# A top-k attention stage: loads split, masked probabilities as a difference of two exponentials, scores in two pairs, weights one turn later

## The reference, cut to what matters

```python
K_TOP = 32                                   # H = 4 heads of DH = 32
Q = (x_text @ Wq).reshape(Bb, Tt, H, DH)     # Tt = 112
K = (x_vision @ Wk).reshape(Bb, Gg, H, DH)   # Gg = 375
scores = jnp.einsum('bthd,bghd->bhtg', Q, K) / np.sqrt(DH).astype(np.float32)
scores = jnp.where(vision_mask[:, None, None, :], scores, -jnp.inf)
topv, topi = jax.lax.top_k(scores, K_TOP)
probs = jax.nn.softmax(topv, axis=-1)
attn = jnp.zeros_like(scores).at[bi, hi, ti, topi].set(probs)
attn_mean = attn.mean(axis=1)
V = x_vision @ Wv
c_t = jnp.einsum('btg,bgd->btd', attn_mean, V)
c_t = c_t * text_mask[..., None]
```

## Time and profile before

| | us |
|---|---|
| median of three runs | 2866.13 |
| the runs | 2863.48 to 2870.03 |
| the profiled execution | 2862.95 |
| its span, first to last instruction | 2861.2 |
| busy in the span: TensorE, Vector engine, ScalarE, GpSimd | 2240.2, 1638.0, 690.7, 736.3 |
| mean granted clock of TensorE | 0.849 of full speed |

### The profile page before, as it was taken

How to read it: one execution, slowest core, us unless ns; L and a number is a source line. 1 busy time by engine, 2 the same in 40 slices (tenths; PEclk the granted TensorE clock), 3 DMA queues, 4 the chain that set the end, 5 groups by cost and what they waited for, 6 DMA issues and landing times.

```text
span 2861.2 us, 36958 instructions
## 1 busy us (share of the span) xinstructions
PE 2240.2 (78%) x14996; PEld 1512.3 (53%) x14996; DVE 1638.0 (57%) x3176; ACT 690.7 (24%) x1321; POOL 736.3 (26%) x667
## 2 busy tenths in 40 slices
PE   4444589899987999699999999988656765775776
PEld 1111245555555666578888888777444543343432
DVE  5888844444443333355555555566298896645335
ACT  4222123223221121122222222222122221211122
POOL 1222269524130000334343434332200001101000
PEclk8666689788887899899999999999756576887888
DMA  2000010000001000100000100100140011300000
GB/s 84 0 0 0 17 66 14 9 9 9 9 13 45 0 1 1 70 1 1 37 22 1 58 1 1 43 1 1 51 93 28 25 33 31 72 19 0 0 0 26
DMA packets 49704, 64.14 MB, mean 22 GB/s; under 512 B 30856, under 2 KB 46976, under 8 KB 48384
## 3 DMA queue, kind: packets, MB, share of 16 engines
q1 hardware_dynamic: 49536, 61.78, 7.4%
HBM read 59.71 MB, written 2.06 MB: 22 GB/s over the span
## 4 chain that ended last, share of the span: by engine, by line
PE 67%; DVE 20%; DMA 4%; POOL 3%; ACT 3%; issue 2%; SPq 1%; POOLq 0%; DVEq 0%; ACTq 0%
PE PS L1200 7%; PE PS L1216 7%; PE PS L617 4%; DVE st_h L478 4%; PE PS L957 4%; PE PS L936 3%; PE PS L1117 3%; DMA ctx_k<-in_ctx 3%; PE PS L1722 3%; DVE st_h L487 2%; PE PS L643 2%; PE PS L1837 2%; PE PS L628 2%; PE PS L656 2%; DVE ln_st L260 2%
## 5 line engine op out<-in xcount | busy, mean ns | idle before, releaser
L279 POOL TENSOR_SCALAR ln_ve<-ln_mv 128x2 f32<-128x2 f32 (+1 forms) x95 | 21.1, 222 | 1631.0 <-DVE ln_mv L263 1630.9
L1392 DVE TENSOR_TENSOR p_x<-PS,cols 128x1024 f32<-128x1024 f32 x112 | 129.3, 1217 | 147.8 <-PE PS L1162 147.8
L333 PE MATMUL PS<-bc_parts,ident 96*128 96x448 bf16 x256 | 88.2, 438 | 159.7 <-DVE st_h L487 149.7
L1454 POOL TENSOR_TENSOR q_x<-q_f,cols 128x2048 f32<-128x2048 f32 x56 | 208.5, 3743 | 9.9 <-ACT q_f L1312 9.9
L800 DVE TENSOR_REDUCE XD<-PS 112x2 f32<-112x750 f32 x128 | 120.3, 940 | 130.8 <-PE PS L643 130.7
L643 PE MATMUL PS<-k_s,q_s 32*112 32x375 f32 x512 | 130.6, 565 | 42.0 <-DVE XD L800 41.2
L769 ACT ACTIVATE e_t<-PS 125x672 f32<-125x672 f32 x128 | 93.6, 731 | 256.3 <-PE PS L656 256.2
L333 PEld LDWEIGHTS PS<-bc_parts,ident 96*128 96x128 bf16 x256 | 22.1, 107 | 235.3 <-DVE st_h L487 192.7
L1021 DVE SCALAR_TENSOR_TENSOR XA<-PS,gate_w,XA 112x256 f32<-112x256 f32 x128 | 61.9, 484 | 135.4 <-PE PS L957 135.4
L530 POOL TENSOR_TENSOR st_h<-st_h 128x448 f32<-128x448 f32 x64 | 71.9, 1135 | 248.8 <-DVE st_h L487 248.4
L656 PE MATMUL PS<-q_s,k_s 32*125 32x112 f32 x1536 | 128.7, 301 | 1.1 <-ACT e_t L769 1.1
(11 more groups left out here) (337 smaller groups left out, 5006.0 us busy)
## 6 DMA issues: line engine op xcount, KB each, us to landing
t_ring<-k_scratch SPq DMA_DIRECT2D x8, 784.0 KB, 12.5
enc_w<-in_enc_w SPq DMA_DIRECT2D x2, 3072.0 KB, 10.0
wc<-in_enc_w SPq DMA_DIRECT2D x2, 3072.0 KB, 11.9
ctx_k<-in_ctx SPq DMA_DIRECT2D x16, 281.2 KB
wc<-in_wc SPq DMA_DIRECT2D x1, 4096.0 KB, 14.6
enc_rows<-in_enc_rows SPq DMA_DIRECT2D x4, 896.0 KB, 12.3
XD<-k_scratch SPq DMA_DIRECT2D x4, 784.0 KB, 9.1
ctx_t<-in_ctxT SPq DMA_DIRECT2D x16, 187.5 KB, 2.4
```

The source lines that it names most:

```text
L333: last = pe.matmul(ps[2 * (j % 2) + m][:, 0:QT], ident16[0:96, s:s + 1].to_broadcast([96, P]), bc_parts[0:96, q * QT:(q + 1) * QT], start= ...
L1392: last = dve.tensor_tensor(p_x[:, m, :, :, :], ps[1][:, m * P:(m + 1) * P].rearrange("p (h i) -> p h i", i=16).unsqueeze(2) .to_broadcast( ...
L1454: last = pool.tensor_tensor(q_x[:, c, :, :].rearrange("p t (h i) -> p t h i", i=16), q_f[:, k % 2, c, :].rearrange("p (t i) -> p t i", i=1 ...
```

## The change

It does the following.

- **Loads.** `features(b)` issues the two `ctx_f` loads on semaphores of their own. They wait for the keys of b - 2, and stand one batch ahead of `ctx_k` in the queue. `keys` waits for `ctx_f` alone, and the second product for `ctx_k`. Five tap tables are loaded in the stage and eleven after it, with the slots in another order.
- **Probabilities.** The Vector engine no longer multiplies. ScalarE computes `e_r`, the exponentials of what turn 3 left in `w_s` (where the 32 marked ones come out as zero), and the exponentials of the 32 found values in `top8`, with their sum in `e_sum`. GpSimd subtracts `e_r` from `e_p`, which leaves the 32 probabilities. `w_s` and `top8` have a place for each head.
- **Weights.** The reciprocal and the scaling of batch b - 1 (`weights`) stand in turn 1 of batch b's first pair, and the diagonals (`spread`) behind the first two exponentials of b.
- **Order on TensorE.** scores(b+1) for heads 0 and 1, context(b-1), scores(b+1) for heads 2 and 3, keys(b+2), then values.

The diff, with most of the unchanged lines left out:

```diff
@@ -145,9 +145,9 @@
         k_e = sb("k_e", [P, 2, S2], pool=s4a)
-        w_s = sb("w_s", [T, 2, S2], pool=s4a)
         e_p = sb("e_p", [T, 2 * XH, S2], pool=s4a)
-        top8 = sb("top8", [T, 2, 4, 8], pool=s4a)
+        top8 = sb("top8", [T, XH, 4, 8], pool=s4a)
+        e_top = sb("e_top", [T, 2, 32], pool=s4a)
         neg_m = sb("neg_m", [T, 4], pool=s4a)
...
@@ -166,6 +166,9 @@
         s4x.close()
+        flat_b = wb[:, :, :].rearrange("p k d -> p (k d)")
+        w_s = flat_b[0:T, 0:XH * S2].rearrange("t (h s) -> t h s", h=XH)
+        e_r = wc[0:T, 5250 + T:5250 + T + 2 * S2].rearrange("t (z s) -> t z s", z=2)
         m1 = XD
...
@@ -181,8 +184,8 @@
             a[0:T, 0:TD * T].rearrange("p (i t) -> p i t", t=T)
-            for a in (wb[:, :, :].rearrange("p k d -> p (k d)"), wc[:, 6144:8192], flat_d[:, 0:TD * T],
-                      flat_d[:, TD * T:2 * TD * T])]
+            for a in (wc[:, 6144:8192], flat_d[:, 0:TD * T], flat_d[:, TD * T:2 * TD * T],
+                      wb[:, :, :].rearrange("p k d -> p (k d)"))]
         SLOTS_T = len(t_slots)
...
@@ -1599,13 +1602,16 @@
         t_loaded = [(sem(f"t_loaded{i}"), 0) for i in range(4)] + [
-            (enc_loaded[0], 64), (enc_loaded[1], 64), (ctx_loaded[0], 16 * B), (ctx_loaded[1], 16 * B)]
+            (enc_loaded[0], 64), (enc_loaded[1], 64), (ctx_loaded[0], 32 * B), (ctx_loaded[1], 32 * B)]
         (m_ready, m_used, x_s_ready, x_first, x_exp, x_rs, x_dg, fi_ready, fi_used, x2_normed, x2_affine,
...
             "g_done f2x_ready f2x_added").split())
+        x_cut, CUT_0 = max_done, PAIRS
+        x_total, SUM_0 = exp_done, PAIRS
+        x_masked, MASKED_0 = pair_added, 8 * len(UNITS)
         S4_ROWS = ("g_in", "b_in", "bf_in", "bf_out", "g_ffn", "b_ffn", "b2", "g_out", "b_out")
...
@@ -1635,34 +1641,43 @@
                 .then_inc(em_loaded, 16)
+
+            def features(b):
+                if b >= 2:
+                    sp.wait_ge(m_ready, m_count("k", b - 2) + 1)
+                for i in range(2):
+                    sp.dma_start(ctx_f[0:CR[i], b % 2, i, :], dr["ctxT"][b, i * P:i * P + CR[i], :])\
+                        .then_inc(ctx_loaded[b % 2], 16)
+
+            features(0)
             for b in range(B):
+                if b + 1 < B:
+                    features(b + 1)
                 if b >= 2:
                     sp.wait_ge(m_ready, m_count("m1", b - 2) + 1)
-                for i in range(2):
-                    sp.dma_start(ctx_f[0:CR[i], b % 2, i, :], dr["ctxT"][b, i * P:i * P + CR[i], :])\
-                        .then_inc(ectx_loaded[b % 2], 16)
                 sp.dma_start(ctx_k[:, b % 2, :, :], dr["ctx"][b].rearrange("(j p) f -> p j f", p=JR))\
...
                     sp.wait_ge(k_stored, 16)
-                    for j in range(6):
+                    for j in range(5):
                         sp.dma_start(t_slots[j], toeplitz(j)).then_inc(t_loaded[j][0], 16)
             sp.wait_ge(m_ready, len(M_AT))
-            for j in range(6, TAPS):
+            for j in range(5, TAPS):
                 if j >= SLOTS_T:
...
         def m_uses():
-            uses = [("q", q) for q in range(NQ)] + [("k", 0)]
-            for b in range(B):
-                if b + 1 < B:
-                    uses.append(("k", b + 1))
-                uses += [("at", b), ("m1", b)]
-                if b % QB == QB - 1:
-                    uses += [("ct", 2 * (b // QB)), ("ct", 2 * (b // QB) + 1)]
+            uses = [("q", q) for q in range(NQ)] + [("k", 0), ("k", 1)]
+            for b in range(B + 1):
+                if b >= 1:
+                    uses += [("at", b - 1), ("m1", b - 1)]
+                if b + 2 < B:
+                    uses.append(("k", b + 2))
+                if b % QB == 0 and b >= 1:
+                    uses += [("ct", 2 * (b // QB) - 2), ("ct", 2 * (b // QB) - 1)]
             return {u: n for n, u in enumerate(uses)}
...
@@ -1695,15 +1710,15 @@
                 bank = m_claim(pe, "k", b)
-                pe.wait_ge(ectx_loaded[b % 2], 48 * (b // 2 + 1))
+                pe.wait_ge(ctx_loaded[b % 2], 32 * (B // 2 + b // 2 + 1))
                 for i in range(2):
...
-            def scores(b):
+            def scores(b, h0):
                 pe.wait_ge(m_used, m_count("k", b) + 1)
-                for h in range(XH):
+                for h in (h0, h0 + 1):
                     n = XH * b + h
...
@@ -1717,6 +1732,7 @@
                 pe.wait_ge(x_dg, b + 1)
+                pe.wait_ge(x_masked, MASKED_0 + XH * (b + 1))
                 for j in range(JC):
...
@@ -1725,6 +1741,7 @@
                 pe.wait_ge(m_used, m_count("at", b) + 1)
+                pe.wait_ge(ectx_loaded[b % 2], 16 * (b // 2 + 1))
                 for i in range(2):
...
@@ -1742,14 +1759,20 @@
             keys(0)
-            scores(0)
-            for b in range(B):
+            keys(1)
+            scores(0, 0)
+            scores(0, 2)
+            for b in range(B + 1):
                 if b + 1 < B:
-                    keys(b + 1)
-                    scores(b + 1)
-                context(b)
-                if b % QB == QB - 1:
-                    values(b // QB)
+                    scores(b + 1, 0)
+                if b >= 1:
+                    context(b - 1)
+                if b + 1 < B:
+                    scores(b + 1, 2)
+                if b + 2 < B:
+                    keys(b + 2)
+                if b % QB == 0 and b >= 1:
+                    values(b // QB - 1)
...
@@ -1885,26 +1908,50 @@
-            copy_keys(0)
-            copy_keys(1)
-            for b in range(B):
-                for h in range(XH):
-                    n = XH * b + h
-                    act.wait_ge(x_first, n + 1)
-                    if b >= 2 and h == 0:
-                        act.wait_ge(m_ready, m_count("at", b - 2) + 1)
-                    act.activation(e_p[:, XH * (b % 2) + h, :], ps[h][0:T, 0:S2], ACT.Exp,
-                                   bias=neg_m[:, h:h + 1]).then_inc(x_exp, 1)
-                    if b >= 1 and h == 1:
-                        copy_attention(b - 1)
-                        copy_context(b - 1)
-                        if b + 1 < B:
-                            copy_keys(b + 1)
+            def exp_all(b, h):
+                n = XH * b + h
+                act.wait_ge(x_first, n + 1)
+                if b >= 2 and h == 0:
+                    act.wait_ge(m_ready, m_count("at", b - 2) + 1)
+                act.activation(e_p[:, XH * (b % 2) + h, :], ps[h][0:T, 0:S2], ACT.Exp,
+                               bias=neg_m[:, h:h + 1]).then_inc(x_exp, 1)
+
+            def exp_rest(b, h):
+                n = XH * b + h
+                act.wait_ge(x_cut, CUT_0 + n + 1)
+                if n >= 2:
+                    act.wait_ge(x_masked, MASKED_0 + n - 1)
+                    act.wait_ge(x_total, SUM_0 + 2 * (n - 1))
+                act.activation(e_r[:, n % 2, :], w_s[:, h, :], ACT.Exp, bias=neg_m[:, h:h + 1]).then_inc(x_total, 1)
+                act.activation(e_top[:, n % 2, :], top8[:, h, :, :].rearrange("t k j -> t (k j)"), ACT.Exp,
+                               bias=neg_m[:, h:h + 1], accum_out=e_sum[:, b % 2, h:h + 1]).then_inc(x_total, 1)
+
+            def spread(b):
                 act.wait_ge(x_rs, b + 1)
...
                 last.then_inc(x_dg, 1)
+
+            copy_keys(0)
+            copy_keys(1)
+            for b in range(B):
+                exp_all(b, 0)
+                exp_all(b, 1)
+                if b >= 1:
+                    spread(b - 1)
+                exp_rest(b, 0)
+                exp_rest(b, 1)
+                exp_all(b, 2)
+                exp_all(b, 3)
+                if b >= 1:
+                    copy_attention(b - 1)
+                    copy_context(b - 1)
+                if b + 2 < B:
+                    copy_keys(b + 2)
+                exp_rest(b, 2)
+                exp_rest(b, 3)
+            spread(B - 1)
             copy_attention(B - 1)
...
@@ -1933,8 +1980,14 @@
             dve.wait_ge(xa_copied, B // 2)
+
+            def weights(b):
+                dve.wait_ge(x_total, SUM_0 + 2 * XH * (b + 1))
+                link(dve.reciprocal(e_rs[:, b % 2, :], e_sum[:, b % 2, :]))
+                dve.tensor_scalar(e_rs[:, b % 2, :], e_rs[:, b % 2, :], tmk[:, b:b + 1], 1.0 / XH,
+                                  ALU.mult, ALU.mult).then_inc(x_rs, 1)
+
             for b in range(B):
-
                 for h0 in range(0, XH, 2):
...
@@ -1947,32 +2000,29 @@
                                 link.after(cut[a])
-                            s = ps[h][0:T, 0:S2] if turn == 0 else w_s[:, a, :]
-                            found[a] = link.mark(dve.max(top8[:, a, turn, :], s))
+                            s = ps[h][0:T, 0:S2] if turn == 0 else w_s[:, h, :]
+                            if turn == 0 and b >= 1:
+                                dve.wait_ge(x_total, SUM_0 + 2 * (n - 3))
```

(28 more changed lines are left out.)

## The result

| | before | after |
|---|---|---|
| median of four runs, us | 2866.88 | 2844.64 |
| the runs, us | 2863.48 to 2870.03 | 2841.04 to 2847.66 |
| ratio to before (95% interval) | | 0.9922 (0.9904 to 0.9941) |
| the profiled execution, us | 2862.95 | 2847.12 |

What follows compares the result with a forecast made beforehand. A DMA chained to TensorE's whole batch work bounded the kernel at 20.9 us a step. Fifteen steps of 18.3, 16.6 for the last batch and 13.2 for values gave 304.3 against 330.1, net -24.2: 2842 us, range 2812 to 2866.

Steps and rivals of the forecast that it cites:

- The load left the chain: Scoring stage: with loads split, the DMA and its issues leave the chain of waits, 6.2 us of a step.
- The masks left the Vector engine: Vector engine, each pair of heads: the mask-and-sum of 1.05 us is removed, with its wait for ScalarE.
- its floor of 16.4 us a batch: Vector engine's own work per batch if nothing else waits: two pairs at 7.99 us plus 0.42 for reciprocal and scaling.
- the price of two heads' scores: TensorE, a pair of heads' scores in the loop: 1.45 us at the full clock, 1.9 at the low one.
- the ring: Loop from `weights` to the next through Vector engine, ScalarE and TensorE: 15.8 us at 2.4 GHz, 19.0 at 1.2 GHz.
- The weighted sum on the chain in most steps: Scoring stage, a sign that the forecast is wrong: most steps wait for the weighted sum, behind `x_masked`.
- 0 to 3 us of waiting a step: Vector engine, a sign that the forecast is right: its waits, all at `weights`, for ScalarE.
- Values: Batches 4, 8 and 12: values' matmuls 3.83 us and last copy 0.53 on the loop, 4.4 each, 13.2 us in all.
- The last batch: End of the scoring stage: 16.6 us, plus 1.1 for the weighted sum beginning later after the last replacement.
- Half the steps at each clock: Scoring steps: half at 16.4 us (full clock), half at 19.0 (low), each plus 0.6; 18.3 us on average.
- The hold: GpSimd's subtraction delaying `neg_m` and `weights`: 0 to 1.3 us a step, 0.6 taken; rival with larger holds, chance 0.10.
- the earlier start: Start of the scoring stage: forecast +0.5 us, waiting for two key products instead of one but for a shorter load.

Runs made afterwards that it cites:

- the last kernel: Changed kernel with four heads' scores between weighted sum and second product, keys' and values' copies late, and values spread over two batches: 2792.78 us, ratio 0.9728.
- The four-head kernel: Changed kernel with the scores of all four heads in one piece behind context(b-1), instead of two pairs: 2825.16 us, ratio 0.9856.
- all of it: Changed kernel with four heads' scores in one piece and the copies of keys and values behind exp_rest: 2808.96 us, ratio 0.9806.

## Why the prediction was right, and where it was wrong

**Right.** The load left the chain: none of the DMAs is waited for, and `features(3)` was issued at 2092.6 us (forecast near 2096). The masks left the Vector engine, and its floor of 16.4 us a batch stands, as the last kernel shows. MAX8 and the replacements keep their 0.53 to 0.54 us beside GpSimd. A pair of `exp_rest` takes 1.7 us (forecast 1.75, with the sum's read at 0.19 us where 0.05 was taken, but the parts overlap), and a subtraction 0.915 (1.0). That the clock would hold the steps apart, in two kinds, is right as well: 16.4 and 20.6 us.

**The step that failed: the price of two heads' scores, and with it what the ring runs through.** I took a pair at 1.2 GHz as "half of 3.8", 1.9 us. It takes 2.78, and 3.2 ahead of the weighted sum. The 2.9 us at 2069.19 I took for the full clock; the granted clock there was 0.50, as the windows view of the kernel before has it:

```profile
2069.19:2072.10 2.91, 2.91 (x17) 1.28 (x17) 0.00 (x0) 0.00 (x0) 2.64 (x4) 0.50 1.00 369
```

So four heads cost 2.8 to 2.9 us at the low clock when nothing stands between them, and the 3.8 us of the earlier trace rows is the same work issued in the rhythm of the exponentials that free its banks. Halving either row is wrong, since the heads of one set read different groups of 32 rows and overlap: four heads take 1.51 us and two 1.45 at the full clock, 2.81 and 2.78 at the low one. The 1.45 us of the forecast was right only by two errors that cancel.

The Trainium skill (TensorE: Matmul & The Clock Gate, Part 3, the packing of small matmuls) says this: matmuls with 32 rows in different row groups run at the same time, and four of them are about three times as fast as one after another. The four-head kernel agrees with it, 2.81 us for four against 2.78 for two; halving the number of heads then saves little, and I hadn't applied it.

With the pair at 2.78 the ring that I had written down, through `weights`, comes to 19.9 us at the low clock. The measured 20.6 us go by another way: the first pair of scores waits for ScalarE's first exponential, which stands behind `copy_keys` and `exp_rest`, and the weighted sum stands behind that pair. I had let the weighted sum begin 2.7 us after `weights`; it begins 3.8 us after it (2207.07 to 2210.84) and takes 5.3, so it ends half a microsecond behind the fourth exponential instead of beside it. The price of the pair alone didn't make this way the longest, as the kernel with the keys copied late shows: the order of ScalarE's work had its part. "The weighted sum on the chain in most steps" was one of the signs for wrong, though behind the scores and not behind `x_masked`. The forecast of 0 to 3 us of waiting a step fails with it: 45.8 us in nine waits, up to 11.3.

**Smaller terms.** *Values* were priced at 3.83 us from one row; at the low clock they take 7.17 us, twice in the stage. *The last batch* was priced only up to the weighted sum. Behind it the clock stayed at 0.50, so the second product took 2.92 instead of 1.63 and values 7.22 instead of 3.83: that is the 4.7 us. It belongs to the clock of that execution and isn't shown to belong to the change: the kernel without the subtraction has the same order of work and took 14.9 us from the last replacement to the last `c_t`, at a granted clock of 0.77, where the changed one took 20.7 at 0.50. *Half the steps at each clock* was near: of the twelve steps without values seven took 15.9 to 16.8 us and five 20.0 to 20.6. *The hold* of 0.6 us a step was half there (0.34 us at the scaling, nothing at `neg_m`) and off the path: taking it away gave 2 us, within what the measurement can tell from nothing.

The Trainium skill (SBUF — State Buffer, Who interferes with whom) says that an instruction of the Vector engine with at most one SBUF input and outside the two-port modes doesn't contend with GpSimd, and that a tensor_scalar can enter such a mode where its operands meet the conditions. The trace agrees for MAX8 and the replacement, and for the scaling, 0.73 us beside a subtraction against 0.23 without. `neg_m`, a TENSOR_SCALAR of a single column, stayed at 0.13 to 0.16 us beside GpSimd, so it wasn't held; which condition it misses no run here shows.

**What made the total come out all the same.** Errors of both signs, and luck. The twelve steps without values took 216.9 us against a forecast of 219.6: the slow ones are 1 us longer than forecast (20.6 against 19.6), the fast ones shorter (16.4 on average against 17.0). The three with values took 77.2 against 68.1, and the tail 4.7 us that had no term. With the earlier start, the profiled execution is 8.3 us above its forecast. The median is only 2.6 us above, because that execution is the longest but one of the four: the median lies 2.5 us below it, where the forecast had put it 3.2 above. These 5.7 us are luck.

That the late copies and the four heads share the blame is shown by each alone (-28.2 with the keys copied late, -27.0 with the values' copies late as well, and -19.5 us against the change) and by all of it (-35.7). Which part of the 20.6 us ring each takes out can't be read as a sum, since the ring changes its way. Not tried: the change's two pairs with the first of them behind the weighted sum.

## What to carry to other kernels

Before splitting a set of matmuls, find out whether its members run side by side: then half a set can cost as much as the whole, as it did here at either clock. A row read at one clock mustn't stand for the other, so read the granted clock of every duration that goes into a sum. When work moves to another engine, follow its queue all the way round, including which bank or buffer its last instruction frees; here the place of one copy on an engine that is busy 40% of the time was worth 28 us, more than the whole change had gained. And run the simplest part of a change alone: here the loads by themselves beat the whole.

## What the hardware showed that I had not expected

- Two heads' scores take 2.78 us at 1.2 GHz and four take 2.81; at 2.4 GHz two take 1.45 and four 1.51.
- A TENSOR_SCALAR of 112x4 beside a GpSimd subtraction takes 0.73 us instead of 0.23, one of 112x1 stays at 0.14 on average. The hold cost nothing that the runs can tell.
- Unused matmuls raised the granted clock of the stage from 0.59 to 0.80 and made the kernel 21.5 us faster than without them, though TensorE then did 79 us more of them.
- A sum on ScalarE is an instruction of its own, 0.188 us, that overlaps the end of the exponential it belongs to.
- The stretch from the last replacement to the last `c_t` took 20.7 us in the changed kernel, at a granted clock of 0.50, and 14.9 us in the one without the subtraction, at 0.77, though both issue the same matmuls in the same order.
